# A conditional two-layer block on one core: the two-layer kinds move to the buffers of the third layer, and one store moves ahead of a subtraction

## What is computed

```
out_nr  = gelu(x @ w1_nr + b1_nr) @ w2_nr + b2_nr
out_tsr = gelu(x @ w1_tsr + b1_tsr) @ w2_tsr + b2_tsr
out_sr  = gelu(gelu(x @ w1_sr + b1_sr) @ w2_sr + b2_sr) @ w3_sr + b3_sr      # w1_sr is 256 x 512
out = where(c == 0, out_nr, where(c == 1, out_tsr, where(c == 2, out_sr, 0)))
y = layernorm(x + out) * gamma + beta
hidden = gelu(y @ down_W.T + down_b)
hidden = hidden @ expert_W[d].T + expert_b[d] + domain_emb[d]
result = layernorm(hidden @ up_W.T + up_b + y) * ln_gamma + ln_beta
```

## Time and profile before

| | |
|---|---|
| time, median of 3 runs | 265.09 us (264.93 to 265.20) |
| the profiled execution | 264.93 us, of which the span of the trace is 263.07 |
| granted clock of PE, mean over the span | 0.989 |
| busy in the span | PE 94%, PEld 84%, DVE 79%, ACT 73%, POOL 67% |
| the chain that ended last | PE 71%, issue 9%, DVE 7%, POOL 7%, ACT 2%, DMA 1% |

### The profile page before, as it was taken

One profiled execution on the slowest core, in us unless ns is written; L12 is line 12 of the kernel. 1 busy time (PEld: TensorE's weight loads), 2 busy tenths in 40 slices (PEclk: granted clock), 3 DMA queues, 4 the chain that ended last, 5 costly groups with the idle time before them and its releaser, 6 DMA issues.

```text
span 263.1 us, 7973 instructions
## 1 busy us (share of the span) xinstructions
PE 247.6 (94%) x2114; PEld 219.9 (84%) x2115; DVE 207.2 (79%) x717; ACT 190.8 (73%) x450; POOL 177.4 (67%) x188
## 2 busy tenths in 40 slices
PE   7998999999999998899999999999999999999860
PEld 6698898989989988797889999988899998888630
DVE  6769633553944945988999999999999999999993
ACT  3578488587696696568888787888877888877640
POOL 3134464374777768678788887878888787877451
PEclk9999999999999999999999999999999999999995
DMA  6372021011122022132333333332333333322215
GB/s 197 90 268 65 12 45 31 15 44 31 34 65 60 20 79 60 40 95 72 93 89 86 92 91 95 85 100 80 90 90 90 90 100 89 90 81 72 58 44 123
DMA packets 41640, 20.71 MB, mean 79 GB/s; under 512 B 37431, under 2 KB 39181, under 8 KB 41614
## 3 DMA queue, kind: packets, MB, share of 16 engines
q1 hardware_dynamic: 37625, 12.10, 19.0%
q0 software_dynamic: 2592, 7.08, 7.7%
q10 hardware_dynamic: 1396, 1.19, 1.7%
HBM read 11.69 MB, written 8.65 MB: 77 GB/s over the span
## 4 chain that ended last, share of the span: by engine, by line
PE 71%; issue 9%; DVE 7%; POOL 7%; ACT 2%; DMA 1%; DVEq 1%; POOLq 0%; ACTq 0%
PE ps_h L1085 19%; PE ps_z L1153 11%; PE ps_u L1205 10%; PE ps_z L1158 5%; PE ps_z L1120 5%; PE ps_t L1175 5%; PE ps_d L1218 4%; PE ps_u L1120 4%; POOL h_lo L482 3%; POOL rs L489 3%; PE ps_t L1256 2%; PE ps_t L1259 2%; PE ps_t L1257 2%; DVE o L770 1%; PE ps_u L1042 1%
## 5 line engine op out<-in xcount | busy, mean ns | idle before, releaser
L482 POOL TENSOR_TENSOR h_lo<-h,h_hi 128x256 fp32r<-128x256 f32 (+1 forms) x75 | 73.3, 978 | 36.4 <-ACT h L908 36.1
L915 ACT ACTIVATE zn<-ps_z,nm,rs 128x256 f32<-128x256 f32 x66 | 33.7, 562 | 33.9 <-DVE nm L707 33.4
L489 POOL TENSOR_TENSOR rs<-ve,minus_half 128x4 f32<-128x4 f32 (+1 forms) x38 | 38.2, 1006 | 26.6 <-DVE ve L703 26.3
L691 DVE BATCH_NORM_STATS2 st<-ps_z 128x6 f32<-128x256 f32 x66 | 24.8, 415 | 32.8 <-PE ps_z L1158 32.8
L908 ACT ACTIVATE h_hi<-ps_h,per_feature_sb 128x256 fp32r<-128x256 f32 x84 | 38.8, 495 | 8.7 <-issue 4.7
L908 ACT ACTIVATE h<-ps_h,per_feature_sb 128x256 f32<-128x256 f32 x84 | 39.0, 501 | 0.0
L508 POOL DMA_INDIRECT out<-o,out_rows_now x27 | 34.6, 1281 | 4.8 <-issue 4.8
L942 ACT ACTIVATE yt<-ps_t,per_feature_sb 128x256 f32<-128x256 f32 x66 | 34.1, 577 | 2.9 <-issue 1.5
L1205 PE MATMUL ps_u<-tables,stack 65*64 x132 | 35.6, 392 | 0.3 <-ACT stack L926 0.3
L1205 PE MATMUL ps_u<-second_table,stack 65*64 65x256 f32 x132 | 35.6, 392 | 0.0
L1153 PE MATMUL ps_z<-last_hi,h_hi 128*128 (+1 forms) x132 | 35.4, 303 | 0.0
(11 more groups left out here) (150 smaller groups left out, 653.2 us busy)
## 6 DMA issues: line engine op xcount, KB each, us to landing
x<-in_x_feat SPq DMA_DIRECT2D x130, 64.0 KB
out<-o SPq DMA_DIRECT2D x18, 64.0 KB, 2.0
out<-o,out_rows_now POOLq DMA_INDIRECT x54
last_sb<-in_last_w SPq DMA_DIRECT2D x1, 768.0 KB, 4.6
w_sr_sb<-in_w_sr SPq DMA_DIRECT2D x1, 512.0 KB, 3.4
w_sr_sb<-in_w_sr ACTq DMA_DIRECT2D x1, 512.0 KB, 4.3
w_two_sb<-in_w_two SPq DMA_DIRECT2D x1, 512.0 KB, 5.7
out<-o ACTq DMA_DIRECT2D x6, 64.0 KB, 2.6
```

Of the source, the lines that this page charges most:

```text
L482: pool.tensor_tensor(dst, full, high.bitcast(F32), ALU.subtract).then_inc(ready, 1)
L489: pool.tensor_tensor(RS[p][:, norms, :], VE[p][:, norms, :], half_of_two[:, norms, :], ALU.pow).then_inc(rstd, 1)
L915: ins = act.activation(ZN[:, t, :], ZP[p][:, t, :], ACT.Identity, bias=NM[p][:, t:t + 1], scale=RS[p][:, 0, t:t + 1])
```

## The change

It does three things.

1. A two-layer slot keeps its hidden values in `h2`, `h2h`, `h2l` (blocks 0 and 1) in place of `h1`, `h1h`, `h1l`. `last_layer` then reads h2 for every kind and loses two arguments.
2. On ACT, within the branch for two-layer slots, there is a further `If(g < b_sr)`. It is true only in the transition: there `residual_norm` comes first, and the GELU of half 0 waits for `z_ps` of the SR slot, whose `last_layer` still reads h2. Otherwise the order is as before, behind one more comparison.
3. On POOL, the transfer of tile 1 moves into both branches. For an SR slot it stands between `powers` and the `low` of half 1, in steps 4 to 7. For two-layer slots it stays behind the `low` of half 1.

```diff
--- before.py
+++ after.py
@@ -514,12 +514,6 @@
                 row = bass.IndirectOffsetOnAxis(ap=OUT_NOW[p][:, 0:1], axis=0)
                 pool.indirect_dma_start(out_rows, row, O[p][:, 0, :], None).then_inc(sc_out[p], 16)
 
-            def store(g, where):
-
-                if where in (MAIN, LAST2):
-                    store_tile1(g - 4, p)
-                    store_tile0(g - 4, p)
-
             def scale(slot, q, p, count):
 
                 pool.wait_ge(rstd, count)
@@ -550,14 +544,19 @@
                 with pool.If(g + 1 < b_sr):
                     low(h1l[:, 0:2, :], h1[:, 0:2, :], h1h[:, 0:2, :], h0_full, h0_lo, g + 1)
                     powers(g, i, p, where)
+                    if where in (MAIN, LAST2):
+                        store_tile1(g - 4, p)
                     low(h1l[:, 2:4, :], h1[:, 2:4, :], h1h[:, 2:4, :], h1_full, h1_lo, g + 1)
                 with pool.Else():
                     for slot in on_slot(g, -1, where):
-                        low(h1l[:, 0, :], h1[:, 0, :], h1h[:, 0, :], h0_full, h0_lo, g + 1)
+                        low(h2l[:, 0, :], h2[:, 0, :], h2h[:, 0, :], h0_full, h0_lo, g + 1)
                     powers(g, i, p, where)
                     for slot in on_slot(g, -1, where):
-                        low(h1l[:, 1, :], h1[:, 1, :], h1h[:, 1, :], h1_full, h1_lo, g + 1)
-                store(g, where)
+                        low(h2l[:, 1, :], h2[:, 1, :], h2h[:, 1, :], h1_full, h1_lo, g + 1)
+                    if where in (MAIN, LAST2):
+                        store_tile1(g - 4, p)
+                if where in (MAIN, LAST2):
+                    store_tile0(g - 4, p)
                 if where in SECOND_ALONE:
                     power(SECOND_ALONE[where] + g, 1 - p, SECOND)
 
@@ -976,15 +975,17 @@
                     with act.If(g < b_sr):
                         act.wait_ge(h2_ps, g + 1)
                         gelu(h2[:, :, :], h2h[:, :, :], [TP[:, 0, :], TP[:, 1, :]], COL_B2_SR, h2_hi, h2_full)
-                def first_of_two(kind):
-
+                def first_of_two(kind, last_read):
+
+                    if last_read:
+                        act.wait_ge(z_ps, g + 1)
                     act.wait_ge(h0_ps, g + 2)
-                    gelu(h1[:, 0:1, :], h1h[:, 0:1, :], [H0[:, 0, :]], 2 * kind, h0_hi, h0_full)
+                    gelu(h2[:, 0:1, :], h2h[:, 0:1, :], [H0[:, 0, :]], 2 * kind, h0_hi, h0_full)
 
                 def second_of_two(kind):
 
                     act.wait_ge(h1_ps, g + 2)
-                    gelu(h1[:, 1:2, :], h1h[:, 1:2, :], [H1[:, 0, :]], 2 * kind + 1, h1_hi, h1_full)
+                    gelu(h2[:, 1:2, :], h2h[:, 1:2, :], [H1[:, 0, :]], 2 * kind + 1, h1_hi, h1_full)
 
                 with act.If(g + 1 < b_sr):
                     act.wait_ge(h0_ps, g + 2)
@@ -998,12 +999,19 @@
                     kind = [kind_of(act, slot) for slot in on_slot(g, -1, where)]
                     if where == HEAD and g < 0:
                         weight_high("w1_two")
-                        first_of_two(kind[0])
+                        first_of_two(kind[0], False)
                     else:
-                        for k in kind:
-                            first_of_two(k)
-                        for slot in on_slot(g, 1, where):
-                            residual_norm(slot, q, where)
+
+                        with act.If(g < b_sr):
+                            for slot in on_slot(g, 1, where):
+                                residual_norm(slot, q, where)
+                            for k in kind:
+                                first_of_two(k, True)
+                        with act.Else():
+                            for k in kind:
+                                first_of_two(k, False)
+                            for slot in on_slot(g, 1, where):
+                                residual_norm(slot, q, where)
                     for k in kind:
                         second_of_two(k)
                     next_input(g, i, p, where)
@@ -1140,7 +1148,7 @@
                         pe.wait_ge(zn_act, g)
                     residual(ZP[q], input_tile(q)).then_inc(x_used, 1)
 
-            def last_layer(kind, high, low, highs, lows, p):
+            def last_layer(kind, highs, lows, p):
 
                 def rows(half, c):
                     return half[:, bass.ds(kind * LW + c * H, H)]
@@ -1150,12 +1158,12 @@
                 for t in range(TT):
                     for c in range(KC):
                         for half in (WH["last"], WL["last"]):
-                            pe.matmul(ZP[p][:, t, :], high[:, c, t * P:(t + 1) * P], rows(half, c),
+                            pe.matmul(ZP[p][:, t, :], h2h[:, c, t * P:(t + 1) * P], rows(half, c),
                                       start=False, stop=False)
                 lows()
                 for t in range(TT):
                     for c in range(KC):
-                        ins = pe.matmul(ZP[p][:, t, :], low[:, c, t * P:(t + 1) * P], rows(WH["last"], c),
+                        ins = pe.matmul(ZP[p][:, t, :], h2l[:, c, t * P:(t + 1) * P], rows(WH["last"], c),
                                         start=False, stop=(t == TT - 1 and c == KC - 1))
                 ins.then_inc(z_ps, 1)
 
@@ -1287,7 +1295,7 @@
                 for slot in on_slot(g, 1, where):
                     transposes(slot, where)
                 weights_ready(where, g, "last")
-                last_layer(SR, h2h, h2l, lambda: None, lambda: pe.wait_ge(h2_lo, g + 1), p)
+                last_layer(SR, lambda: None, lambda: pe.wait_ge(h2_lo, g + 1), p)
                 for slot in on_slot(g, 2, where):
                     expert(slot, p, where, at[0])
 
@@ -1296,7 +1304,7 @@
                 for slot in on_slot(g, 0, where):
                     weights_ready(where, g, "last")
 
-                    last_layer(kind, h1h, h1l, lambda: pe.wait_ge(h1_hi, g + 1), lambda: pe.wait_ge(h1_lo, g + 1), p)
+                    last_layer(kind, lambda: pe.wait_ge(h1_hi, g + 1), lambda: pe.wait_ge(h1_lo, g + 1), p)
                 start_two(g, 1 - p, where)
                 adapter(g, p, where)
```

## The result

The changed kernel takes 267.64 us (median; 267.12 to 269.02 in four runs) against 265.01 for the kernel before on the same chip (264.52 to 265.20): 1.0108 times as long, with a 95% interval of 1.0079 to 1.0138. The ratio is taken over more runs than these medians, fourteen of the changed kernel, and leaves out the only run of any kernel that fell out of the common state (407.83 us at a granted clock of 0.559, with one comparison on ACT). The forecast was 266.0, 1 us slower; it is 2.6 slower, just beyond the upper end of the range (267.6). The profiled execution took 267.34, of which the span is 265.5; before, these were 264.93 and 263.07, so the two traces differ by 2.41.

A forecast was written before the change was run, and what follows sets the result against it. PE was taken to set the pace, with 0.03 us slack per two-layer step. Terms 0.36 + 0.16 + 0.32 + 0.15 = 0.99 us on 264.93 gave 265.92, plus 0.16 for the median: 266.0 us, range 265.2 to 267.6.

The forecast's parts named there:

- The sign and the transition: Whole kernel slower, chance 0.70; in step 8, ACT's wait for z_ps delays the low PE waits for, costing 0.32 us.
- Edit 2: Store of tile 1 ahead of the low of half 1, SR steps 4 to 7: 0 in steps 4 to 6, 0.15 us in step 7.
- the overlap of the low with DVE: SR steps: low meets two o, then blocks the bias additions; low ends at 91.2, x at 91.8, PE needs x at 91.82.
- rival (b): SR steps 4 to 7: POOL loses the port to DVE after L508, 0.6 + 0.3 more, 266.9 up to 267.6; chance 0.12.
- Step 7: PE wants h_lo one group (1.4 us) sooner; x is ready at 101.9 where PE went on at 101.75: 0.15 us, at most 0.45.
- The comparison in the two-layer stage: ACT's extra comparison before h_hi behind the loop's edge delays h_lo, costing PE 0.04 at nine edges: 0.36 us.
- The price of a comparison: On ACT in the two-layer branch: 0.16 us, taken from a POOL comparison that jumps; bounds 0.04 and 0.38.
- the slack behind it: Two-layer stage: h_lo can be 0.03 us late per step before PE waits; 0.09 more was left by the overlap.
- Rival (c): ACT's sequencer takes the comparison while the engine still works; only the transition pays, 0.47: 265.5; chance 0.16.
- The tail: First step behind the loop has no air, so ACT's comparison is paid in full: 0.16 us, bounds 0.04 and 0.38.

## Why the forecast was right and wrong

**The sign and the transition: right.** The wait for `z_ps` costs 0.35 (0.32 forecast) for the forecast's reason. The changed kernel's rows answer to the earlier trace rows, POOL and then PE:

```profile
109.49 0.73 POOL L482 TENSOR_TENSOR h_lo<-h,h_hi 128x256 fp32r<-128x256 f32 x1 [2.60 <-ACT h L907]
110.32 1.04 POOL L489 TENSOR_TENSOR rs<-ve,minus_half 128x4 f32<-128x4 f32 x1
111.35 1.12 POOL L482 TENSOR_TENSOR h_lo<-h,h_hi 128x256 fp32r<-128x256 f32 x1
```

```profile
112.52 0.74 PE L1166 MATMUL ps_z<-last_hi,h_lo 128*128 x4 [1.17 <-POOL h_lo L482]
```

From `z_ps` (108.36) to the power is 1.96; before it was 107.30 - 105.69 = 1.61.

**Edit 2 in SR steps 4 to 6: wrong, and this is where most of the miss lies** (1.84 against 0). The step of the prediction that failed is the overlap of the low with DVE: "low meets DVE's two o and then the two bias additions ... Low starts in earnest near 89.9 and ends at 91.2, x at 91.2 + 0.6 = 91.8". It let the two `o` pass before the low took hold, because they start while the store still runs, and charged only the bias additions with waiting. The runs show the reverse. The low takes hold of what DVE starts while the low is still only next in line (2.75 in place of 0.87 for the two `o`; 0.87 again as soon as another store stands between), and the low itself isn't slowed at all (1.31). So `x` comes not 0.6 behind the low's end but behind the rest of the first `o`, a second `o` and two additions: 93.73 - 92.48 = 1.25. Counted from `z_ps`, x was forecast at 91.8 - 85.77 = 6.0 and came at 93.73 - 87.05 = 6.7, and that difference is about the 0.61 that PE's weight load waits and the 0.56 by which steps 5 and 6 grew. The forecast's rival (b), "the SR steps pay too", said 0.6 + 0.3 for this and was given 0.12; its mechanism was another (DVE keeps POOL from the port), and it was the wrong way round: it is POOL that keeps DVE off. The Trainium skill (SBUF — State Buffer, Who interferes with whom) had named the pair, an instruction of DVE with two SBUF inputs and a GpSimd one that reads SBUF, and `o` is one; the forecast quoted it and then applied it only to what overlaps in the rows. That was the error.

**Step 7: the place was right, the size wrong** (0.83 against 0.15). h_lo was forecast at 101.3 - 95.88 = 5.42 behind `z_ps`, and PE took it at 103.17 - 97.72 = 5.45. The rest is `x` again, 0.7 later than forecast, as in steps 4 to 6: that term is 0.15 + 0.68.

**The comparison in the two-layer stage: wrong** (0.00 against 0.36). The price of a comparison, 0.16, and the slack behind it were right; that the two older jumps on the same path would get 0.14 cheaper was not to be seen in the trace of before. ACT idles 0.39 before h_hi behind the loop's edge in the changed kernel, where 0.54 was forecast. (`x_lo`, which the forecast calls a copy, is a subtraction with two inputs in SBUF; its sum doesn't hang on that.) Rival (c), hidden by ACT's sequencer, gives the same time for another reason, so it would have been right by luck. The Trainium skill (Advanced Engine Details and Errata, Control Flow Timing) has about 108 ns for a compare-and-branch; here it was 0.15 to 0.16, and 0.24 and 0.22 for two of them in the kernel before, so no one figure holds. **The tail: the first term right** (0.20 against 0.16), **the rest missed**: the same comparison frees DVE's table copies 5 us later and gives 0.53 back.

**The sum.** 1.84 + 0.83 + 0.35 + 0.20 + 0.03 - 0.06 - 0.53 - 0.20 = 2.46 between the last events, and 2.41 between the two executions. Forecast was 0.99. With the two holds rightly placed (0.6 in each of steps 4 to 7, 0.5 less at the end) the same sum would have been about 2.9 less the 0.36 for the comparison, 2.5.

## What to carry to other kernels

When an instruction of POOL that reads SBUF is moved, look at what DVE starts in the last 0.8 us ahead of it, not only at what overlaps it: what starts there may be held until it has ended, and whatever else stands behind on DVE is late with it. One store ahead of it on POOL was no cover; a second store was, and one memset in between let one of two instructions through. An added branch has to be priced with the jumps around it, since these can change by almost as much as it costs (0.14 against 0.16); and a fixed order of two instructions on POOL is worth a branch where one step of the kernel differs from the rest, as in the transition (1.1 us by the trace, 0.7 by the runs).

## What the runs showed of the hardware that I had not expected

- The low that is next in POOL's line held DVE's `o` off from 0.75 us before its own start to its end: 2.35 in place of 0.47. With another store between, 0.47. At the end a table copy was held too (0.82 in place of 0.28), with a power ahead of the low that was next, and only until that power's end; in the traces where h came 0.4 behind the start of the power it wasn't held.
- Two comparisons on ACT took 0.24 and 0.22 in one layout of the code and 0.165 and 0.157 in another: the first in all five traces without a further comparison on ACT, the second in all nine with one or more (0.157 to 0.163).
- Behind the same two waits of PE (1.02 and 0.51) the granted clock fell to 0.52 for 3.5 us in one kernel's trace and stayed at 1.00 in another's. It cost 1.5 us. In a third, behind one wait of 2.27, it was 0.50 from 107.8 to 111.2.
